# A graph network's aggregation loops: PE drains every four steps, and its sequencer increments the semaphore in place of the matmul

## The chip, the cores and the metric

The kernel runs on one core of one Trainium2 chip. The metric is the time of the program on the device in microseconds. Three runs of the kernel before took 13378.3, 13381.01 and 13399.08 us; their median is 13381.01 us. Within 0.2% of it is 27 us to either side.

## The reference, cut to what matters

```python
def _gcn_layer(x, src, dst, norm, W, b, n_nodes):
    h = x @ W
    msg = h[src] * norm[:, None]
    out = jax.ops.segment_sum(msg, dst, num_segments=n_nodes)
    return out + b

# x: 12500 x 256 float32; 200000 edges, sorted by dst, and a self edge for each node
x = x + gnn(_layernorm(x), edges)         # three _gcn_layer, gelu behind the first two
x = x + experts(_layernorm(x), edges2)    # attention scores on a second graph pick 2 of 4 experts
```

The change lies in the `segment_sum` of the three layers of the first part.

## The kernel before, in words

The nodes are cut into 98 blocks of 128. Their features (256 float32 each) lie scaled in a table in DRAM, `feature_table`, and the sums are collected in SBUF, in `acc`. The edges are listed as 1664 steps of 128 edges; all edges of a step go to one block. `aggregate(l)` runs once in each of three layers over 52 turns of two halves, each of `U` = 16 steps, so a layer has 104 halves and the three have 312. A finishing stage (`finish`, matmuls with the layer's weights) stands behind each. The two halves of `ring` and of `onehot` take turns. For a half:

- POOL (GpSimd) waits until PE has used this half of the ring (`s_used`), copies 16 columns of indices (L687) and issues 16 indirect DMAs (L691), one for a step; each fetches 128 rows of the table into the ring.
- DVE (VectorE) waits for `s_used` as well and makes the 16 one-hot matrices of the half with one operation, L719 (128x2048, both operands in SBUF), which stands in its program behind the sixteen adds of the half before it.
- PE (TensorE) waits for the rows and for the one-hots, then multiplies, step by step, one-hot by rows into PSUM (L708). A float32 matmul is two passes in the records, so a half has 32. Every `Q` = 4 steps it waits for free PSUM (`s_sum`, L707) and tells DVE that four products are there (`s_mm`, L711). Behind the sixteenth it waits for all of them (L712) and increments `s_used` with its sequencer (L713).
- DVE adds each product to its block in `acc` (L734), four at a time behind a wait for `s_mm` (L732), each behind the one before it; the block numbers are loaded every eight steps (L140, called in L730), and `s_sum` is incremented every four (L739).

The semaphore `s_mm` is the only thing that the change touches. The rest of the program is the layout of the edges in front, an attention stage with loops of its own behind the layers (transposes in L1052, indirect DMAs in L1018) and the experts at the end (matmuls in L1382 and L1397).

Of the kernel before, what the change touches and what calls it, by code (L numbers as in the profile page):

```python
# [22 lines left out]
U = 16  # L23
# [25 lines left out]
def build(nc, x, src, dst, gnn_w, gnn_b, w_gat, att_src, att_dst, b_gat, ln_gamma, ln_beta,  # L49
          ew1, eb1, ew2, eb2, edges2, out):  # L50
    N, D = x.shape
# [22 lines left out]
    with ExitStack() as ctx:  # L74
        def sb(name, shape, dt=F32):
            return ctx.enter_context(nc.sbuf_tensor(name, shape, dt))
# [3 lines left out]
        def sem(name):  # L80
            s = nc.alloc_semaphore(name=name)
            phase_sems.append(s)
            return s
# [12 lines left out]
        ps = ctx.enter_context(nc.psum_tensor("ps", [P, 8, 512], F32))  # L96
# [14 lines left out]
        onehot = sb("onehot", [P, 2, U, P])  # L111
# [26 lines left out]
        def load_blocks(which, i, s, n=8, top=NB - 1):  # L138

            _, values = nc.values_load_multi_w_load_instructions(  # L140
                blk[i][0:1, bass.ds(s, n)], engines=[which], min_val=0, max_val=top,
                skip_runtime_bounds_check_because="the table counts blocks of the graph, made on the chip")
            return values
# [525 lines left out]
        ring = work[:].rearrange("p (h u f) -> p h u f", h=2, u=U)  # L669
        G1 = S1 // (2 * U)  # L670
        Q = 4

        def aggregate(l):
            n = f"_l{l}"
            s_row = [sem(f"rows_in{h}" + n) for h in range(2)]
            s_stg, s_tick = sem("indices_staged" + n), sem("pool_tick" + n)
            s_used = sem("ring_half_used" + n)
            s_hot, s_mm, s_add, s_sum = sem("onehots" + n), sem("products" + n), sem("adds" + n), sem("psum_free" + n)
            with nc.Block() as block:
                @block.gpsimd  # L680
                def _(pool):
                    with pool.Fori(0, G1) as g:
                        for h in range(2):

                            pool.wait_ge(s_used, g * 2 + (h + 1))
                            pool.sem_inc(s_tick, 1)
                            nc.gpsimd.tensor_copy(stage[:, h], idx[0][:, bass.ds(g * (2 * U) + h * U, U)]).then_inc(s_stg, 1)  # L687
                            pool.wait_ge(s_stg, g * 2 + (h + 1))
                            pool.sem_inc(s_tick, 1)
                            for k in range(U):  # L690
                                nc.gpsimd.indirect_dma_start(  # L691
                                    out=ring[:, h, k], out_offset=None, in_=table,
                                    in_offset=bass.IndirectOffsetOnAxis(ap=stage[:, h, k:k + 1], axis=0),
                                ).then_inc(s_row[h], 16)

                @block.tensor
                def _(pe):
                    pe.sem_inc(s_used, 2)
                    with pe.Fori(0, G1) as g:
                        for h in range(2):  # L700
                            pe.wait_ge(s_row[h], (g + 1) * (16 * U))
                            pe.wait_ge(s_hot, g * 2 + (h + 1))
                            for k in range(U):
                                bank = (k // 2) % 8
                                if k % Q == 0:

                                    pe.wait_ge(s_sum, g * (2 * U // Q) + (h * U + k) // Q + 1)  # L707
                                mm = nc.tensor.matmul(ps[:, bank, (k % 2) * D:(k % 2 + 1) * D], onehot[:, h, k],  # L708
                                                      ring[:, h, k], start=True, stop=True, skip_group_check=True)
                                if k % Q == Q - 1:  # L710
                                    mm.then_inc(s_mm, 1)  # L711
                            pe.wait_ge(s_mm, g * (2 * U // Q) + (h + 1) * (U // Q))  # L712
                            pe.sem_inc(s_used, 1)  # L713

                @block.vector
                def _(dve):
                    dve.sem_inc(s_sum, U // Q)
                    def hots(g, h):
                        nc.vector.tensor_tensor(  # L719
                            onehot[:, h], iota[:].unsqueeze(1).broadcast_to([P, U, P]),  # L720
                            dloc[0][:, bass.ds(g * (2 * U) + h * U, U)].unsqueeze(2).broadcast_to([P, U, P]),
                            ALU.is_equal).then_inc(s_hot, 1)
                    with dve.Fori(0, G1) as g:
                        for h in range(2):
                            dve.wait_ge(s_used, g * 2 + (h + 1))
                            hots(g, h)
                            for k in range(U):
                                bank = (k // 2) % 8
                                if k % 8 == 0:
                                    base = load_blocks(mybir.EngineType.DVE, 0, g * (2 * U) + (h * U + k), top=(NB - 1) * D)  # L730
                                if k % Q == 0:
                                    dve.wait_ge(s_mm, g * (2 * U // Q) + (h * U + k) // Q + 1)  # L732
                                at = bass.ds(base[k % 8], D)
                                nc.vector.tensor_tensor(acc[:, at], acc[:, at], ps[:, bank, (k % 2) * D:(k % 2 + 1) * D],  # L734
                                                        ALU.add).then_inc(s_add, 1)

                                dve.wait_ge(s_add, h * U + k + 1)
                                if k % Q == Q - 1:
                                    dve.sem_inc(s_sum, 1)  # L739
                        dve.sem_clear(s_add)  # L740
# [262 lines left out]
        s_hot, s_mm, s_mrg, s_keep = sem("gat_penalties"), sem("gat_scores"), sem("gat_merged"), sem("gat_rows_kept")  # L1003
# [465 lines left out]
```

## Time and profile before

| | |
|---|---|
| median of three runs | 13381.01 us |
| the profiled execution's own time: its span | 14933.7 us |
| the same, core 0's mean granted TensorE clock | 0.702 |
| L691, indirect DMAs on POOL | 4992, 5155.3 us busy |
| L708, matmul passes on PE | 9984, 2933.4 us busy |
| L734, adds on DVE | 4992, 2103.8 us busy |
| L719, one-hots on DVE | 312, 716.4 us busy |

The profiled execution lasted 1553 us (11.6%) longer than the median of the runs. Of its own time no other figure is there than its span. A row of the timeline below gives the start in us, the duration in us, the engine, the line, the operation and how many are merged, and in brackets the idle time before it with what ended it. "remote" and "issue" are idle times for which no instruction of another engine is named. The granted clock is in parts of TensorE's full 2.4 GHz.

### The profile page before, as it was taken

The page shows a single profiled execution, that of the slowest core. Times are in us where ns is not written, and L with a number is a line of the kernel's source. Part 1 is how long each engine was busy: PE and PEld are TensorE (multiplying, and loading weights), DVE is VectorE, ACT ScalarE, POOL GpSimd, SP SyncE. Part 2 cuts the span into 40 slices and gives each one's busy share as a digit, 9 for nine tenths or more (in the row PEclk, how much of TensorE's full clock was granted, in tenths as well). Part 3 has the DMA queues.
Part 4 walks back from the last instruction along what each step waited for, and adds up shares of the span by engine and source line. Part 5 has one row for each costly group of instructions (what it writes and reads, how often), then busy time and mean ns, then how long its engine had stood idle before and what let it go on. Part 6 is the DMA issues. An engine that isn't in the chain of part 4 may idle for free. (4 is left out here: it accounts for less than half of the span.)

```text
span 14933.7 us, 122356 instructions
## 1 busy us (share of the span) xinstructions
PE 6795.4 (46%) x29462; PEld 5570.3 (37%) x29462; DVE 6207.0 (42%) x12229; ACT 2112.3 (14%) x6085; POOL 7853.7 (53%) x8847
## 2 busy tenths in 40 slices
PE   0120034333434334343443334336555555777999
PEld 0120023333323333333333333325333334777888
DVE  8870233333333333333333333335444445553222
ACT  0000000000001000000100000003666664111222
POOL 0387367777765777777477777761545554330000
PEclk9997566676667666666666666666555555558999
DMA  0000133333322333333133333323000000001000
GB/s 8 7 0 5 44 103 88 88 88 88 89 68 73 89 87 88 88 87 88 53 88 90 90 88 90 88 65 94 5 5 5 5 5 4 1 1 33 28 29 27
DMA packets 468304, 809.55 MB, mean 54 GB/s; under 512 B 156361, under 2 KB 306425, under 8 KB 468210
## 3 DMA queue, kind: packets, MB, share of 16 engines
q0 software_dynamic: 309248, 667.09, 16.3%
q1 hardware_dynamic: 158962, 141.56, 3.1%
q14 instruction: 79, 0.65, 0.0%
q8 instruction: 15, 0.25, 0.0%
HBM read 729.01 MB, written 79.15 MB: 54 GB/s over the span
## 5 line engine op out<-in xcount | busy, mean ns | idle before, releaser
L691 POOL DMA_INDIRECT work<-feature_table,stage x4992 | 5155.3, 1033 | 1758.4 <-issue 1575.6
L708 PE MATMUL ps<-work,onehot 128*128 128x256 f32 x9984 | 2933.4, 465 | 5150.6 <-DVE onehot L719 2591.1
L708 PEld LDWEIGHTS ps<-work,onehot 128*128 128x128 f32 x9984 | 2367.5, 241 | 5716.4 <-issue 5274.2
L734 DVE TENSOR_TENSOR acc<-acc,ps 128x256 f32 x4992 | 2103.8, 421 | 4472.5 <-PE ps L708 1772.9
L1052 PE MATMUL ps<-ident,onehot 128*128 128x128 f32 x4608 | 1160.9, 402 | 1105.1 <-ACT onehot L1037 435.8
L1037 ACT ACTIVATE onehot<-work 128x128 f32<-128x128 bf16 x4608 | 1374.5, 387 | 801.8 <-DMA HG<-L_ffn_edge_index_in 635.4
L1052 PEld LDWEIGHTS ps<-ident,onehot 128*128 128x128 f32 x4608 | 767.6, 204 | 1498.1 <-issue 770.9
L1018 POOL DMA_INDIRECT work<-attention_table,stage x1152 | 1106.3, 960 | 405.3 <-issue 349.8
L226 POOL DMA_INDIRECT edge_list<-rec_stage,stage x1024 | 1115.7, 1090 | 369.2 <-issue 309.5
L780 ACT ACTIVATE work<-acc,dinv 128x256 f32 (+1 forms) x294 | 131.6, 496 | 7732.1 <-PEq L794 7539.5
L1075 DVE TENSOR_REDUCE work<-ps 128x4 f32<-128x512 f32 x1152 | 720.6, 684 | 885.0 <-DMA HG<-L_ffn_edge_index_in 652.6
L719 DVE TENSOR_TENSOR onehot<-iota,dloc 128x2048 f32<-128x2048 f32 x312 | 716.4, 2296 | 189.9 <-DVE acc L734 107.4
L1382 PE MATMUL ps<-acc 128*128 128x256 f32 x3136 | 703.4, 380 | 68.4 <-DMA acc<-x_normed_t 68.4
L1397 PE MATMUL ps<-acc 128*128 128x256 f32 x3136 | 700.8, 379 | 0.0
L1382 PEld LDWEIGHTS ps<-acc 128*128 128x128 f32 x3136 | 597.5, 191 | 150.2 <-issue 68.6
L1397 PEld LDWEIGHTS ps<-acc 128*128 128x128 f32 x3136 | 595.8, 190 | 81.0
L1247 POOL COPY work<-work 128x24 bf16 x1152 | 274.2, 289 | 648.6 <-PE ps L1206 592.2
L1437 DVE SCALAR_TENSOR_TENSOR acc<-ps,gates,acc 128x256 f32<-128x256 f32 x392 | 171.7, 479 | 963.2 <-PE ps L1397 963.2
L1014 POOL COPY stage<-idx 128x16 int32 x72 | 15.8, 219 | 966.6 <-PEq L1055 677.1
L803 PE MATMUL ps<-gw_sb,work 128*128 128x256 f32 x1176 | 319.2, 420 | 402.4 <-DVE work L824 258.4
L687 POOL COPY stage<-idx 128x16 int32 x312 | 132.1, 423 | 668.5 <-PEq L713 344.7
L1413 ACT ACTIVATE acc<-ps,acc 128x256 f32<-128x256 f32 x784 | 307.6, 475 | 969.0 <-PE ps L1382 969.0
(202 smaller groups left out, 5302.9 us busy)
## 6 DMA issues: line engine op xcount, KB each, us to landing
work<-feature_table,stage POOLq DMA_INDIRECT x4992
feature_table<-acc SPq DMA_DIRECT2D x98, 256.0 KB
work<-attention_table,stage POOLq DMA_INDIRECT x1152
edge_list<-rec_stage,stage POOLq DMA_INDIRECT x1024
feature_table<-acc SPq DMA_DIRECT2D x7, 1792.0 KB, 6.7
x_after_gnn<-acc SPq DMA_DIRECT2D x49, 256.0 KB
x_normed_t<-work SPq DMA_DIRECT2D x49, 256.0 KB, 2.2
acc<-x_normed_t SPq DMA_DIRECT2D x49, 256.0 KB, 2.8
```

The costliest lines, as they stand in the source:

```text
L226: nc.gpsimd.indirect_dma_start(out=target, out_offset=bass.IndirectOffsetOnAxis(ap=stage[0:rows, h, k:k + 1], axis=0), in_=rec_stage[0:row ...
L691: nc.gpsimd.indirect_dma_start(out=ring[:, h, k], out_offset=None, in_=table, in_offset=bass.IndirectOffsetOnAxis(ap=stage[:, h, k:k + 1], ...
L708: mm = nc.tensor.matmul(ps[:, bank, (k % 2) * D:(k % 2 + 1) * D], onehot[:, h, k], ring[:, h, k], start=True, stop=True, skip_group_check= ...
L719: nc.vector.tensor_tensor(onehot[:, h], iota[:].unsqueeze(1).broadcast_to([P, U, P]), dloc[0][:, bass.ds(g * (2 * U) + h * U, U)].unsqueez ...
L734: nc.vector.tensor_tensor(acc[:, at], acc[:, at], ps[:, bank, (k % 2) * D:(k % 2 + 1) * D], ALU.add).then_inc(s_add, 1)
L803: mm = nc.tensor.matmul(ps[:, 2 + r, a * D:(a + 1) * D], zt[:, r, a, k * P:(k + 1) * P], gw_sb[:, l, k], start=(k == 0), stop=(k == KD - 1 ...
L1018: nc.gpsimd.indirect_dma_start(out=grow[:, h, k], out_offset=None, in_=gat_table, in_offset=bass.IndirectOffsetOnAxis(ap=stage[:, h, k:k + ...
L1037: ins = nc.scalar.activation(pairs4[:, k % 4, j], penal[:, h, k], ACT.Identity, bias=grow[:, h, k, HE + j:HE + j + 1], scale=BIG)
L1052: mm = nc.tensor.transpose(ps[:, bank, j * P:(j + 1) * P], pairs4[:, k % 4, j], ident[:])
L1075: nc.vector.tensor_reduce(mx[:, h, k], ps[:, k % 8].rearrange("p (j e) -> p j e", j=NH), AX.X, ALU.max).then_inc(s_pf, 1)
L1382: mm = nc.tensor.matmul(ps[:, 2 * (e % 2) + m // 2, (m % 2) * 2 * P:(m % 2 + 1) * 2 * P], w1[:, e, k, m * P:(m + 1) * P], xt[:, r, :, k], ...
L1397: mm = nc.tensor.matmul(to, hid[:, e % 2, m, a * P:(a + 1) * P], w2[:, e, m], start=(m == 0), stop=(m == KH - 1), skip_group_check=True)
```

## The change

The last matmul of each four no longer increments `s_mm`. PE is drained there instead, and its sequencer increments `s_mm` with an instruction of its own. The wait for `s_mm` before `s_used` falls away.

```diff
                                 if k % Q == 0:
                                     pe.wait_ge(s_sum, g * (2 * U // Q) + (h * U + k) // Q + 1)
-                                mm = nc.tensor.matmul(ps[:, bank, (k % 2) * D:(k % 2 + 1) * D], onehot[:, h, k],
-                                                      ring[:, h, k], start=True, stop=True, skip_group_check=True)
+                                nc.tensor.matmul(ps[:, bank, (k % 2) * D:(k % 2 + 1) * D], onehot[:, h, k],
+                                                 ring[:, h, k], start=True, stop=True, skip_group_check=True)
                                 if k % Q == Q - 1:
-                                    mm.then_inc(s_mm, 1)
-                            pe.wait_ge(s_mm, g * (2 * U // Q) + (h + 1) * (U // Q))
+                                    pe.drain()
+                                    pe.sem_inc(s_mm, 1)
                             pe.sem_inc(s_used, 1)
```

## Rows read from the trace of the kernel before

**Rows 1.** First and third loop: length, PE, PEld, DVE, ACT, POOL busy, PE clock, DMA

```profile
1904.00:4376.00 2472.00, 963.21 (x3296) 778.16 (x3296) 929.74 (x1747) 0.00 (x0) 1758.40 (x1766) 0.69 0.30 88
...
7453.00:9927.00 2474.00, 980.17 (x3328) 790.70 (x3328) 939.68 (x1768) 0.87 (x3) 1761.93 (x1770) 0.68 0.30 88
```

**Rows 2.** One half in which POOL waits for nobody, timeline from 2094 us

```profile
2094.23 0.21 POOL L687 COPY stage<-idx 128x16 int32 x1
...
2096.26 8.86 PE L708 MATMUL ps<-work,onehot 128*128 128x256 f32 x32 [15.34 <-DMA work<-feature_table,stage]
...
2110.32 0.95 POOL L691 DMA_INDIRECT work<-feature_table,stage  x1 [0.30 <-issue]
...
2115.04 0.20 POOL L687 COPY stage<-idx 128x16 int32 x1
```

**Rows 3.** The last half of the third layer, with its adds on DVE

```profile
9911.42 9.53 PE L708 MATMUL ps<-work,onehot 128*128 128x256 f32 x32 [11.26 <-DMA work<-feature_table,stage]
9915.33 2.08 DVE L734 TENSOR_TENSOR acc<-acc,ps 128x256 f32 x4 [5.04 <-PE ps L708]
9917.72 2.08 DVE L734 TENSOR_TENSOR acc<-acc,ps 128x256 f32 x4 [0.31 <-PE ps L708]
9920.84 2.08 DVE L734 TENSOR_TENSOR acc<-acc,ps 128x256 f32 x4 [1.04 <-issue]
9923.24 2.08 DVE L734 TENSOR_TENSOR acc<-acc,ps 128x256 f32 x4 [0.31 <-DVE acc L734]
```

**Rows 4.** The first half of the first layer: adds, POOL and PE, timeline from 1928 us

```profile
1928.14 9.29 PE L708 MATMUL ps<-work,onehot 128*128 128x256 f32 x32 [643.78 <-DMA work<-feature_table,stage]
...
1951.13 2.08 DVE L734 TENSOR_TENSOR acc<-acc,ps 128x256 f32 x4 [10.15 <-remote]
1951.43 0.20 POOL L687 COPY stage<-idx 128x16 int32 x1 [4.53 <-PEq L713]
```

**Rows 5.** Who waited for whom, in total over the span: us, times, longest

```profile
DVE acc L734 <- remote: 1652.7, 314, 13.9
...
POOL stage L1014 <- PEq L1055: 677.1, 69, 15.4
...
POOL stage L687 <- PEq L713: 344.7, 107, 4.6
```

**Rows 6.** The one-hots of L719 between POOL's DMAs, timeline from 1954 and from 2876 us

```profile
1955.94 2.29 DVE L719 TENSOR_TENSOR onehot<-iota,dloc 128x2048 f32<-128x2048 f32 x1 [0.33 <-DVE acc L734]
1956.24 2.81 POOL L691 DMA_INDIRECT work<-feature_table,stage  x1 [0.30 <-issue]
...
1959.35 0.95 POOL L691 DMA_INDIRECT work<-feature_table,stage  x1 [0.30 <-issue]
...
2876.72 2.29 DVE L719 TENSOR_TENSOR onehot<-iota,dloc 128x2048 f32<-128x2048 f32 x1 [0.83 <-DVE acc L734]
2877.94 1.89 POOL L691 DMA_INDIRECT work<-feature_table,stage  x1 [0.30 <-issue]
2880.14 0.95 POOL L691 DMA_INDIRECT work<-feature_table,stage  x1 [0.30 <-issue]
```

**Rows 7.** A drain behind two matmuls, and PE's sequencer: ns min/median/max

```profile
138.90 0.75 PE L412 MATMUL ps<-work,ones 128*128 128x98 f32 x2 [138.90 <-DVE acc L308]
...
L314 PEldq DRAIN  x2: 795/926/1057, 138.9 to 1014.5; - x2
...
L713 PEldq EVENT_SEMAPHORE  x312: 51/51/51, 1951.1 to 9921.0; - x156
L1140 PEldq DRAIN  x1: 8/8/8, 13505.5 to 13505.5; - x1
```

**Rows 8.** Passes and weight loads: of L708 min/median/max, of L1382 sixteen in a row

```profile
L708 PEld LDWEIGHTS ps<-work,onehot x9984: 190/190/338, 1928.1 to 9920.4; 128*128 128x128 f32 x200
L708 PE MATMUL ps<-work,onehot x9984: 379/379/791, 1928.1 to 9920.6; 128*128 128x256 f32 x200
...
14201.32 3.62 PE L1382 MATMUL ps<-acc 128*128 128x256 f32 x16
```

## The prediction

> **What bounds the kernel now.** Read first the busy times by stretch [rows 1]. In a loop of 2472 us POOL is busy for 1758, PE for 963, DVE for 930, and the DMA engines are at 0.30. POOL carries the most, but no engine is full. The third loop has 2474 us, the second is like them: about 7420 us in all, 23.8 for each of 312 halves.
>
> Then the timeline of one half in which POOL waits for nobody [rows 2]. From copy to copy it takes 2115.04 - 2094.23 = 20.81 us: sixteen indirect DMAs, one every 1.254 us, and about a us for the copy. PE starts on the half that was just fetched 2.03 us behind the copy and is done 8.9 us later (2933.4 us over 312 halves is 9.4 on average, by the table of the page). So PE gives a half of the ring back some 11.4 us into the 20.8 that POOL needs for the other one. The reader is to see 9 us of slack there. The last half of the third layer shows DVE [rows 3]: its first adds begin 3.91 us behind PE, then at 6.30, 9.42 and 11.82, and end at 13.9. Group 1 waits for PE; from there DVE, with 2.4 us a group and 3.1 where block numbers are loaded, is mostly the slower.
>
> What makes 23.8 out of 20.8? Two things. The first is L719 [rows 6]. While DVE builds one-hots for 2.29 us, the next DMA of POOL doesn't end. With L719 0.03 us behind the start of a DMA (2877.94 - 1.25 = 2876.69), the next-but-one starts 2.20 us behind the next in place of 1.25: POOL loses 0.95. With L719 0.95 us behind such a start, it loses 3.11 - 1.25 = 1.86. The loss is thus about 0.92 us plus L719's distance from the last start, 0.92 to 2.17 in all. The second is late signals. In the first half PE's records end at 1937.43, and yet the third group's adds begin at 1951.13, behind a wait for "remote", and POOL's copy is released by PE's sequencer only then [rows 4]. Such waits come to 1652.7 us in 314 cases on DVE, about one a half, and they cost POOL 344.7 us in L687 [rows 5].
>
> The median of the runs is 1553 us under this profiled execution. I read the late signals as belonging to the profiled execution for the greater part: POOL without them would need 20.81 + 1.5 = 22.3 us a half, 6960 in all, which gives back 460; another 677.1 are POOL's waits of the same kind in the attention stage [rows 5]; together 1140 of the 1553, with the other stages left for the rest. That the two sums come near to each other is an argument, not a proof, and the first rival stands on its being false. Under this reading the loops of the runs are bound by POOL's issue.
>
> **The change, part by part.** *Removed.* 1248 increments by matmuls, which occupy nobody, and 312 waits of PE's sequencer before L713, which wait for what the last drain now waits for. Nothing is gained on POOL's path. No DMA moves, and no queue is passed by anything.
>
> *Added: 1248 drains, four a half.* A drain that stands behind two matmuls took 795 ns beside 0.75 us of matmuls, so it ended 0.05 us behind them; one with nothing before it took 8 ns [rows 7]. So it waits for the array and adds 0.05. Then the sequencer's increment takes 0.051 us [rows 7]; with what no row shows of its way to DVE I take the signal to be 0.2 us later than the matmul's own, between 0.05 and 0.4. Then the next group starts anew. The pass behind used to start 0.22 us behind its forerunner (sixteen passes take 3.62 us with the last at 0.38), now it starts behind its end: 0.16 lost at 2.4 GHz. Its weights have to be loaded, 0.19 to 0.34, and the first pass is up to 0.79 [rows 8]. With the sequencer's instructions between I take 0.8 us a group, between 0.45 and 1.2. Three of these gaps lie inside a half: PE needs 9.4 + 2.4 + 0.2 = 12.0 us, and gives back its half of the ring 2.0 + 12.0 = 14.0 us into POOL's 20.8. The cover is 6.8 us. If the gaps keep PE at 1.2 GHz all through, each group takes 3.91 [rows 3] and the half 4 x 3.91 + 3 x 0.8 = 18.0, given back at 20.1: still hidden, now by 0.7 us plus L719's loss of 1.5.
>
> The Trainium skill, in "VectorE: DVE Perf Modes", section "The DRAIN you can't avoid", tells of boilerplate drains of about 12 ns on all engines; by it the 1248 drains would cost 15 us at most, and by the 795 ns row they cost what the array still has to do. Either is hidden under POOL here.
>
> *What is late next.* Behind the waits for `s_mm` on DVE stand the adds and, behind them, L719 of the half that PE has just given back. Nobody waits for that one-hot soon (PE needs it 20 us later), but where L719 falls decides what POOL loses. Now: PE starts 2.03 behind the copy, the last adds begin 11.82 later, and L719 follows 2.08 + 0.33 later, or 2.08 + 0.83 where a turn of the loop lies between [rows 3, 6]: 16.3 or 16.8 us behind the copy, up to 0.5 more where group 2 is late. POOL's thirteenth DMA starts at 2110.32 - 2094.23 = 16.09 [rows 2], the next at 17.34. The distances are 0.2 to 0.7 and 0.7 to 1.2, mostly near the low ends; mean 0.57, loss 1.5 us. After: group 1's signal is 0.2 late, group 2 is bound by PE in place of DVE, 0.2 to 1.5 later in all, taken at 0.8. L719 comes at 17.1 to 17.6 and at 17.6 to 18.1. The first lot is astride the start at 17.34 (distance 1.0 to 1.25, and 0 to 0.25), the second at 0.25 to 0.75. Mean 0.53, loss 1.45. The difference of -0.05 us times 312 is -15 us; with the unknown size of the shift it can be 0.15 to either side, 47 us. At 1.2 GHz throughout, L719 falls around the copy at 20.8; for that place no row of mine differs in kind, and I take a loss between 0.92 and 2.17.
>
> *The tails.* The last half of each layer has no POOL to hide it: three times about 2.6 us on PE, of which DVE's own pace hides 1.8: +3 us, bounds 1 and 15.
>
> Sum: 0 (drains and increments) - 15 + 3 = -12 us, with +15 for the chance of a lower clock moving more of L719 to dear places: 13381 + 3. The sum is made on the trace's halves and laid on the median, since what differs between the two executions, the late waits, isn't in it. I say 13385.
>
> The Trainium skill, in "SBUF — State Buffer", section "SBUF: two separate sides", has DVE operations with two SBUF inputs and GpSimd exclude each other for the whole instruction. By a lock that costs the same wherever it falls, the change would be worth nothing but the tails; the two cases above (0.95 and 1.86 us) show that the place matters, so I keep the 47 us.
>
> **The rivals.** *First, faster: the late signals are real.* If the runs have them too, and the sequencer's increment isn't held up as the matmul's is, POOL no longer waits: 344.7 us in L687 [rows 5], giving 13036; it decides once the signals come less than about 9 us late. For it: 314 waits, one a half. Against: 1553 us have to vanish somewhere, and a drain would wait for the same completion. Chance 0.09.
>
> *Second, faster by place.* The shift carries L719 just past the starts of DMAs more often than I think: -0.3 us a half at most by likelihood, 13290; bound 0.57 x 312 = 178 us. Chance 0.13.
>
> *Third, slower by place.* The shift is 0.3 to 0.5, not 0.8, or the clock stays low: then L719 falls late in a DMA's time, loss 1.75 to 2.0, +0.25 to +0.5 us a half, +80 to +156, typically 13480. It decides from a mean shift of +0.09 us. For it: PE's gaps come at a granted clock of 0.69 already [rows 1], between the two levels. Chance 0.28.
>
> *Fourth, slower by the drain.* A gap of over 1.7 us in place of 0.8, at the low clock, makes PE and not POOL the bound; each us more costs 3 x 312 = 936 us. Against it: the 795 ns row. Chance 0.05, from 13600 up.
>
> **How the numbers follow.** No change, within 0.2% (27 us, about what a measurement of this kernel can tell): 0.45. Faster 0.09 + 0.13 = 0.22. Slower 0.28 + 0.05 = 0.33. The range leaves out the first and the fourth rival and the ends of the other two: 13290 to 13530. My own case alone is 13340 to 13430.
>
> **What the profile of the changed kernel would show.** PE should have 1248 more drains, each behind its matmuls and 0.05 us longer, and gaps of 0.5 to 1.2 us between groups of eight passes; the mean half from first to last pass about 12 us. POOL's undisturbed half should stay at 20.8 us, and the first adds come 4.1 us behind PE. DVE's "remote" waits should stay if they belong to the completion of matmuls; if they vanish while the runs don't move, they were the profile's. L719 should begin 17 to 18 us behind the copy in undisturbed halves. I'm wrong if POOL waits for L713 in an undisturbed half, or if the loops' share of the change is over 0.15 us a half.

## The result and the profile after

The changed kernel took 13439.15 us (median of six runs) beside 13386.03 us for the kernel before (six runs): ratio 1.0038, 95% interval 1.0027 to 1.005. It is 53 us slower. The range of 13290 to 13530 holds the time. What the prediction called its own case alone, 13340 to 13430, misses it by 9 us. The likeliest case, no change beyond 0.2%, didn't come, the side of "slower" did (0.33).

The profiled execution of the changed kernel spans 13439.0 us, as long as its runs. The one of before that the prediction read spanned 14933.7 us. Where that difference comes from, the run before_again shows. Two lines of the changed kernel's page:

```profile
span 13439.0 us, 123604 instructions
...
PE 6900.3 (51%) x29462; PEld 5352.4 (40%) x29462; DVE 6241.2 (46%) x12229; ACT 2094.0 (16%) x6085; POOL 7963.1 (59%) x8847
```

Its waits, of which PE's and DVE's in the loops are shown (us in total, times, longest). No wait of L734 is called remote any more, and POOL's L687 waits for no L713 or L712, where it waited 344.7 us [rows 5]:

```profile
PE ps L708 <- DMA work<-feature_table,stage: 4292.8, 312, 408.6
DVE acc L734 <- PEq L711: 3162.4, 488, 26.7
...
PE ps L708 <- issue: 131.0, 611, 0.2
```

What ran is not quite what the program text says. The text asks for a drain (L711) and for an increment of `s_mm` by an instruction of its own (L712). In the trace the 1248 drains carry the increment, and DVE is released by them, as the line above shows. Of sequencer increments there are 312, one behind each half's fourth drain, under L712, and none under L713:

```profile
L712 PEldq EVENT_SEMAPHORE  x312: 51/51/51, 1702.7 to 9132.8; - x156
```

Those are the increments of `s_used`. The 0.051 us that the prediction gave to an increment of `s_mm` don't occur. Where the texts below speak of sequencer increments of PE for `s_mm`, read drains that increment.

One half of the changed kernel in the timeline:

```profile
6002.68 0.21 POOL L687 COPY stage<-idx 128x16 int32 x1
...
6004.65 3.78 PE L708 MATMUL ps<-work,onehot 128*128 128x256 f32 x8 [11.67 <-DMA work<-feature_table,stage]
...
6008.59 2.08 DVE L734 TENSOR_TENSOR acc<-acc,ps 128x256 f32 x4 [9.23 <-PEq L711]
...
6008.65 2.97 PE L708 MATMUL ps<-work,onehot 128*128 128x256 f32 x8 [0.22 <-issue]
...
6011.78 2.08 DVE L734 TENSOR_TENSOR acc<-acc,ps 128x256 f32 x4 [1.11 <-PEq L711]
...
6019.70 2.29 DVE L719 TENSOR_TENSOR onehot<-iota,dloc 128x2048 f32<-128x2048 f32 x1 [0.33 <-DVE acc L734]
6019.99 2.83 POOL L691 DMA_INDIRECT work<-feature_table,stage  x1 [0.30 <-issue]
6023.12 0.95 POOL L691 DMA_INDIRECT work<-feature_table,stage  x1 [0.30 <-issue]
...
6025.32 0.21 POOL L687 COPY stage<-idx 128x16 int32 x1
```

The reader is to see three things. PE's passes now come in packs of eight with 0.22 us between the modelled end of one and the start of the next. POOL goes on from copy to copy without a wait, in 22.64 us here: 20.81 and 1.83 more, for the DMA that L719 stretched to 2.83 us. And L719 stands 17.02 us behind POOL's copy, 0.96 us behind the start of the last DMA (19.99 - 1.25 = 18.74), a dear place.

### The profile page after: what moved, and what is told of

It is laid out like the page before. It is cut to its first block and busy times, and to the rows that moved or that the text cites. A ratio compares the mean times of both kernels' runs of the same rounds, so it can differ in the third digit from the quotient of the medians.

```text
span 13439.0 us, 123604 instructions
## 1 busy us (share of the span) xinstructions
PE 6900.3 (51%) x29462; PEld 5352.4 (40%) x29462; DVE 6241.2 (46%) x12229; ACT 2094.0 (16%) x6085; POOL 7963.1 (59%) x8847
## 5 line engine op out<-in xcount | busy, mean ns | idle before, releaser
L691 POOL DMA_INDIRECT work<-feature_table,stage x4992 | 5235.6, 1049 | 1759.2 <-issue 1486.2
L708 PE MATMUL ps<-work,onehot 128*128 128x256 f32 x9984 | 3126.9, 467 | 4493.0 <-DMA work<-feature_table,stage 4292.8
L708 PEld LDWEIGHTS ps<-work,onehot 128*128 128x128 f32 x9984 | 2209.9, 233 | 5409.7 <-issue 4833.0
L734 DVE TENSOR_TENSOR acc<-acc,ps 128x256 f32 x4992 | 2102.9, 421 | 4125.5 <-PEq L711 3162.4
L1018 POOL DMA_INDIRECT work<-attention_table,stage x1152 | 1196.3, 1038 | 405.0 <-issue 348.0
L1052 PE MATMUL ps<-ident,onehot 128*128 128x128 f32 x4608 | 1113.9, 388 | 562.8 <-ACT onehot L1037 490.3
L1052 PEld LDWEIGHTS ps<-ident,onehot 128*128 128x128 f32 x4608 | 734.4, 197 | 942.0 <-issue 646.8
L719 DVE TENSOR_TENSOR onehot<-iota,dloc 128x2048 f32<-128x2048 f32 x312 | 715.7, 2294 | 323.2 <-DVE acc L734 171.8
L1382 PE MATMUL ps<-acc 128*128 128x256 f32 x3136 | 702.4, 380 | 68.8 <-DMA acc<-x_normed_t 68.8
L1382 PEld LDWEIGHTS ps<-acc 128*128 128x128 f32 x3136 | 596.8, 190 | 150.3 <-issue 68.9
L1413 ACT ACTIVATE acc<-ps,acc 128x256 f32<-128x256 f32 x784 | 307.6, 475 | 968.0 <-PE ps L1382 968.0
L1180 DVE TENSOR_TENSOR acc<-acc,ps 128x20 f32 x1152 | 201.8, 175 | 257.0 <-DVE acc L1180 222.4
L1082 DVE TENSOR_TENSOR emx<-emx,work 128x4 f32 x1152 | 190.5, 165 | 268.6 <-DVE work L1075 124.3
```

Of the source, the lines that this page charges most:

```text
L691: nc.gpsimd.indirect_dma_start(out=ring[:, h, k], out_offset=None, in_=table, in_offset=bass.IndirectOffsetOnAxis(ap=stage[:, h, k:k + 1], ...
L719: nc.vector.tensor_tensor(onehot[:, h], iota[:].unsqueeze(1).broadcast_to([P, U, P]), dloc[0][:, bass.ds(g * (2 * U) + h * U, U)].unsqueez ...
L1018: nc.gpsimd.indirect_dma_start(out=grow[:, h, k], out_offset=None, in_=gat_table, in_offset=bass.IndirectOffsetOnAxis(ap=stage[:, h, k:k + ...
L1052: mm = nc.tensor.transpose(ps[:, bank, j * P:(j + 1) * P], pairs4[:, k % 4, j], ident[:])
L1382: mm = nc.tensor.matmul(ps[:, 2 * (e % 2) + m // 2, (m % 2) * 2 * P:(m % 2 + 1) * 2 * P], w1[:, e, k, m * P:(m + 1) * P], xt[:, r, :, k], ...
L1413: ge = nc.scalar.activation(hid[:, e % 2, m], ps[:, 2 * (e % 2) + m // 2, (m % 2) * 2 * P:(m % 2 + 1) * 2 * P], ACT.Gelu, bias=b1[:, e, m: ...
```

## The experiments

Each experiment ran beside the kernel before on the same chip, and the chips were of two kinds: on some, before takes 13383 to 13386 us, as in the result; on others 14774 to 14793 us, and the trace has late signals as in [rows 4]. Every ratio below is to the kernel before on the same chip, and I call the two kinds punctual and late.

The theories: A, the change costs what L719's later place costs POOL. B, the late signals belong to increments by matmuls and not to the profile. C, it costs by the number of drains or sequencer increments. D, L719's place costs nothing. E, on late chips the drain waits for the late completion and PE with it; F, the drain escapes it. G, the cost goes through PE or its clock.

**before_again** (late chip), the kernel before with no edit.

> The kernel before, unchanged, with a profile of its own. Both theories: the time is that of before within 0.2%, which shows what a comparison can tell. Theory A (place of L719): the profiled execution now lasts about 13385 us, without the late signals; POOL's period is about 22.5 us a half (22.64 in the changed kernel, less 0.16), the second adds of a half begin 6.3 to 6.4 us behind PE's first pass on average against 6.50 in the changed kernel, and L719 begins about 0.15 us earlier behind the copy than its 16.6 to 16.7 us there. Theory B (late signals belong to matmul increments): the profiled execution shows them again, with waits called remote on nearly every half.

Measured: 14793.14 us, ratio 1.0002 (0.9993 to 1.0011); profiled span 14800.3. The same kernel takes 1407 us more here than beside the result, and its waits are those of the trace that I predicted from:

```profile
DVE acc L734 <- remote: 1420.4, 291, 14.0
...
POOL stage L1014 <- PEq L1055: 608.6, 64, 15.2
...
POOL stage L687 <- PEq L713: 314.8, 98, 4.6
```

So the late signals are in the unprofiled runs too, on such a chip. My reading of them as part of the profiled execution is refuted, and with it the forecast of a profile of about 13385 us.

The loops have less than a quarter of the difference. Against the trace of drain_last (below, punctual) this one is longer by 231 us ahead of the first loop, 330 in the three loops, 204 in the finishing stages between them, 644 behind the third loop, and by about 1 in the experts' stage at the end (worked out from the starts of L687 and L1382 and the ends of L734). Nor are only the increments of `s_mm` late: the finishing stage has waits of the same name, up to 32.5 us, which the changed kernel's trace from a punctual chip hasn't:

```profile
DVE work L819 <- remote: 330.7, 14, 32.5
```

**drains_only** (late chip):

```diff
                                 if k % Q == Q - 1:
                                     mm.then_inc(s_mm, 1)
+                                    pe.drain()
```

> Drains every four steps, but the matmuls still increment. Theory A: what costs is the restart of PE behind the first drain, which delays group 2 and by it L719; the signal of the sequencer itself is only 0.02 us later. So nearly all of the change is here: +35 to +55 us. Theory C (the sequencer's increments cost, four a half, through a signal that comes later): less than 15 us of the 53 are here.

Measured: 14978.51 us, ratio 1.0123 (1.01 to 1.0146). On a late chip drains alone cost 186 us, far more than either forecast, both of which were made for a punctual one. By far the greater part of the change's cost is in the drains there, since the whole change costs 1.36% (below); C, which had it in the increments, falls on a late chip.

**late2** and **late9** (late chip): two and nine increments of a spare semaphore by DVE's sequencer, ahead of L719.

```diff
                             dve.wait_ge(s_used, g * 2 + (h + 1))
+                            for _ in range(9):
+                                dve.sem_inc(s_late, 1)
                             hots(g, h)
```

> The kernel before, with two sequencer increments of DVE (about 0.1 us each) ahead of L719 and nothing on PE. Theory A: L719 starts 0.2 us later in each half, POOL loses 0.2 us more in most of 312 halves, +45 to +65 us, like the changed kernel. Rival D (what the change costs lies in PE, not in L719's place): no change, within 15 us, since DVE is free for 8 us a half.

> The kernel before, with nine such increments ahead of L719, about 0.86 us. Theory A: the distance of L719 from the start of POOL's last DMA wraps past 1.254 us in most halves, from about 0.5 to 0.1, so POOL loses less: 0.3 to 0.4 us a half, -60 to -125 us against before. Rival D: no change or a few us more, since the delay is hidden. A rival with a loss that only grows with the delay: +0.86 x 312 = +268 us.

Measured: 14783.88 us, 0.9992 (0.9983 to 1.0001), and 14764.02 us, 0.9985 (0.9976 to 0.9994). Both forecasts missed: late2 gave no loss, late9 22 us of gain by the ratio, where -60 to -125 was expected. Late signals scatter L719 over POOL's half there: in the trace of before_again it starts within 5 us behind a copy in 122 halves and over 16 us behind it in nearly all others, so a delay can't set its distance from a DMA's start; these two runs speak neither for A nor for D on a punctual chip.

**after_again** (late chip), the changed kernel with no further edit.

> The changed kernel, unchanged, beside the kernel before. Where before takes some 13386 us: 1.0038 again (+40 to +65 us). Where before takes some 14790 us, because signals of matmuls come late: theory E (the drain waits for the same late completion, and now PE itself stands in it before each next group) +1% or more, as drains alone gave +1.23% there; theory F (only the increment of a matmul is late, the drain is not) a gain of 2 to 4%, since POOL's waits for L713 vanish.

Measured: 14973.95 us beside 14774.45, ratio 1.0136 (1.0115 to 1.0156). That is theory E; F is refuted. The drains' own durations (ns, min/median/max), first of the changed kernel on the punctual chip, then here:

```profile
L711 PEldq DRAIN  x1248: 1832/1988/3777, 1692.2 to 9130.7; - x179
```

```profile
L711 PEldq DRAIN  x1248: 1970/3738/14452, 1923.7 to 10097.9; - x179
```

A drain lasts as long as the eight passes ahead of it, 1.99 or 3.78 us; on the late chip it lasts up to 14.45. Then PE stands where it would have gone on with the next group, and POOL waits 556.9 us for its half of the ring in this trace, in place of 314.8 in before_again:

```profile
POOL stage L687 <- PEq L712: 556.9, 121, 11.3
```

The timeline of that trace shows PE standing 7.14 us between two groups:

```profile
6001.56 1.99 PE L708 MATMUL ps<-work,onehot 128*128 128x256 f32 x8 [0.27 <-issue]
...
6010.64 2.08 DVE L734 TENSOR_TENSOR acc<-acc,ps 128x256 f32 x4 [7.06 <-PEq L711]
...
6010.69 3.78 PE L708 MATMUL ps<-work,onehot 128*128 128x256 f32 x8 [7.14 <-issue]
```

**drain_first** (late chip): as drains_only, but one drain a half, where `k == Q - 1`.

> The kernel before with one drain a half, behind the fourth step; all increments by matmuls. Theory A where signals are punctual: group 2 is the one whose signal binds DVE, so this drain alone costs most of the change, +30 to +55 us. Rival C (sequencer increments cost): 0. Where signals are late: below the +1.23% of four drains, about a quarter of it, since the wait behind the first group is the one that is least often late.

Measured: 14813.31 us, ratio 1.0029 (1.0017 to 1.0041), a quarter of four drains' 1.23%, as expected for a late chip.

**act_hots_before** and **act_hots_after** (late chip, twice each): ACT makes the one-hots and L719 is gone from DVE. The core of the edit; act_hots_after has the change's drains and increments besides.

```python
act.wait_ge(s_used, g * 2 + (h + 1))
nc.scalar.activation(negated[:, h], dloc[0][:, bass.ds(g * (2 * U) + h * U, U)],
                     ACT.Copy, scale=-1.0).then_inc(s_neg, 1)
act.wait_ge(s_neg, g * 4 + (2 * h + 1))
for k in range(U):
    far = nc.scalar.activation(onehot[:, h, k], iota[:], ACT.Abs, bias=negated[:, h, k:k + 1])
far.then_inc(s_neg, 1)
act.wait_ge(s_neg, g * 4 + (2 * h + 2))
nc.scalar.activation(onehot[:, h].rearrange("p u m -> p (u m)"),
                     onehot[:, h].rearrange("p u m -> p (u m)"),
                     ACT.Relu, bias=ones[:, 0:1], scale=-1.0).then_inc(s_hot, 1)
```

> The kernel before, but ACT makes the one-hots (sixteen Abs of iota minus the place, then one Relu of 1 minus it), DVE has no L719. Theory A (L719's overlap costs POOL 0.92 to 2.17 us a half): where signals are punctual POOL's period falls from 22.5 to 20.81 us, 312 x 1.7 = -530 us, about 12860. Rival D (L719 costs POOL nothing on the path): within 30 us of before. Where signals are late: -300 to -530 us.

> The same with the change's drains and sequencer increments. Theory A: with L719 gone there is nothing that a later DVE could push, so the change costs only its tails: within 10 us of act_hots_before where signals are punctual. Rival G (the change costs through PE, its sequencer or the granted clock): 40 to 60 us more than act_hots_before, as on the kernel before.

Measured: 14743.9 us, ratio 0.9979 (0.997 to 0.9987), and 15497.1 us, ratio 1.049 (1.0475 to 1.0504). The gain of 300 to 530 us didn't come, but the stretched DMAs went. Here are POOL's indirect DMAs (ns, min/median/max), with L719 on DVE in before_again and then without it in act_hots_before:

```profile
L691 POOL DMA_INDIRECT work<-feature_table,stage x4992: 942/946/3063, 1901.0 to 9833.9; - x200
```

```profile
L693 POOL DMA_INDIRECT work<-feature_table,stage x4992: 942/949/1007, 1898.5 to 9764.4; - x200
```

Not one of the 4992 is over 1.01 us any more, and a half in which POOL waits for nobody takes 20.77 us, though PE, DVE and now ACT work beside it:

```profile
6018.24 0.20 POOL L689 COPY stage<-idx 128x16 int32 x1 [4.94 <-PEq L715]
...
6039.01 0.20 POOL L689 COPY stage<-idx 128x16 int32 x1
```

So it is L719 on DVE that stretches the DMAs: with the same one-hots made on ACT, and all else of the loop in place, none is stretched. The time stays because on a late chip POOL waits instead: 700.0 us for PE's increment of `s_used`, in place of 314.8. ACT's first operation of a half waits for PE instead (4180.4 us in 235 cases), and DVE for signals (3002.1 us, 368 cases, longest 20.3):

```profile
ACT negated L722 <- PEq L715: 4180.4, 235, 32.4
DVE acc L745 <- remote: 3002.1, 368, 20.3
```

Theory A's forecast of +10 us at most for the drains, made for a punctual chip, isn't tested by this. The drains cost far more with ACT's one-hots, 15497 against 14744; they last up to 18.9 us:

```profile
L713 PEldq DRAIN  x1248: 1923/3352/18927, 1917.5 to 10547.9; - x179
```

**after_late9** (punctual chip): late9's edit on the changed kernel.

> The changed kernel with nine sequencer increments of DVE ahead of L719, which start it 0.84 us later. Theory A where signals are punctual: the distance from POOL's last DMA start goes from mostly 0.5 to 1.2 us on by 0.84 and past 1.254 in nearly all halves, to 0.1 to 0.8; POOL loses 0.3 to 0.5 us less a half, -95 to -155 us against the changed kernel, which makes it 40 to 100 us faster than before. Rival D (L719's place costs nothing): +50 us against before, as the change alone. Where signals are late: within 0.3% of the changed kernel there, +1.1 to +1.6% against before.

Measured: 13365.45 us beside 13383.41, ratio 0.9984 (0.9975 to 0.9993). The changed kernel goes from 1.0038 to 0.9984 by nothing but idle instructions on DVE: 72 us, where 95 to 155 was forecast. It beats the kernel before by 18 us (0.16%), where 40 to 100 was forecast. A has the direction, with sizes forecast too large; rival D is refuted. L719 stands 0.77 us later on average than in the changed kernel (17.45 us behind the copy against 16.69), and POOL loses 0.21 us less a half, 67 of the 72 us (worked out over 306 halves as below). Its timeline, another half than the ones above:

```profile
6006.11 0.95 POOL L692 DMA_INDIRECT work<-feature_table,stage  x1 [0.30 <-issue]
6006.35 2.29 DVE L720 TENSOR_TENSOR onehot<-iota,dloc 128x2048 f32<-128x2048 f32 x1 [1.63 <-issue]
6007.36 2.10 POOL L692 DMA_INDIRECT work<-feature_table,stage  x1 [0.30 <-issue]
6009.76 0.94 POOL L692 DMA_INDIRECT work<-feature_table,stage  x1 [0.31 <-issue]
```

The one-hots stand 0.24 us behind the DMA's start and the next DMA lasts 2.10, not 2.83: POOL loses 1.15 us (2.40 from start to start less 1.25), not 1.88 (3.13 less 1.25) as in the half of the changed kernel above.

**drain_last** (same punctual chip): one drain a half, at its end, which carries the increment as in the changed kernel.

```diff
-                                if k % Q == Q - 1:
+                                if k % Q == Q - 1 and k < U - 1:
                                     mm.then_inc(s_mm, 1)
-                            pe.wait_ge(s_mm, g * (2 * U // Q) + (h + 1) * (U // Q))
+                            pe.drain()
+                            pe.sem_inc(s_mm, 1)
```

> The kernel before with one drain and one sequencer increment a half, behind the sixteenth step, in place of that matmul's increment and of the wait before L713. Theory A where signals are punctual: DVE is behind PE there, and PE has nothing to start, so within 10 us of before. Rival C (sequencer increments or drains cost by their number): a quarter of the change, +13 us. Theory E where signals are late: PE waited for that completion before too, so within 0.15% of before, against +1.23% for drains behind all four groups. Rival F (the drain escapes the late completion): a gain of over 1%.

Measured: 13385.15 us, ratio 0.9997 (0.9988 to 1.0006). One drain with its increment where nothing follows is free within the noise; a cost by number of a quarter of the change (+0.1%) is only just outside the interval. The profile of this kernel is the nearest that I have to one of before on a punctual chip. Its three loops and POOL's busy time in them (windows from the first copy of a layer to its last add; the columns as in [rows 1]):

```profile
1669.00:4018.00 2349.00, 958.34 (x3328) 776.59 (x3328) 939.09 (x1768) 0.00 (x0) 1744.27 (x1767) 0.69 0.32 93
4193.00:6559.00 2366.00, 979.60 (x3328) 790.80 (x3328) 939.18 (x1768) 0.00 (x0) 1761.02 (x1768) 0.69 0.32 92
6735.00:9092.00 2357.00, 975.23 (x3328) 788.40 (x3328) 939.01 (x1768) 0.00 (x0) 1751.92 (x1767) 0.69 0.32 93
sum 7072.00, PE 2913.17 PEld 2355.78 DVE 2817.28 ACT 0.00 POOL 5257.20; mean PE 971.06 PEld 785.26 DVE 939.09 ACT 0.00 POOL 1752.40
```

The same of the changed kernel:

```profile
1668.00:4040.00 2372.00, 1037.08 (x3328) 733.92 (x3328) 939.01 (x1767) 0.00 (x0) 1767.62 (x1768) 0.72 0.32 92
4216.00:6586.00 2370.00, 1045.26 (x3328) 738.74 (x3328) 939.65 (x1768) 0.00 (x0) 1765.09 (x1768) 0.72 0.32 92
6762.00:9136.00 2374.00, 1044.52 (x3328) 737.27 (x3328) 939.31 (x1768) 0.00 (x0) 1768.95 (x1768) 0.72 0.32 92
sum 7116.00, PE 3126.86 PEld 2209.93 DVE 2817.97 ACT 0.00 POOL 5301.66; mean PE 1042.29 PEld 736.64 DVE 939.32 ACT 0.00 POOL 1767.22
```

The loops are 44 us longer of the 49 by which the spans differ (13439.0 and 13390.4), and POOL's busy time is longer by the same 44 us (5301.66 - 5257.20), DVE's by less than 1. The time is inside POOL's DMAs, and what lengthens those is L719, as act_hots_before showed. That speaks against G too: PE is 214 us longer busy in these loops, but POOL waits for it in neither.

**act_hots_before_2** and **act_hots_after_2** repeated the ACT pair, for a punctual chip, and met a late one.

> One-hots made by ACT, increments by the matmuls, once more, for a chip on which signals are punctual. Theory A there: POOL's period falls from the 22.5 us of the run with one drain a half to 20.81 us, 312 x 1.69 = -527 us, about 12860; POOL's DMAs are 0.95 us in every half. Rival D: within 30 us of before. Where signals are late: -0.2% again.

> The same with the change's drains and sequencer increments. Theory A where signals are punctual: PE is 9.4 to 10.6 us busy of 20.81 a half and no L719 is there to be pushed, so within 15 us of the run above. Rival G (the change costs through PE, its sequencer or the granted clock and not by L719's place): +40 to +60 us on the run above. Where signals are late: +4.9% again, by theory E.

Measured: 14758.25 us, ratio 0.9977 (0.9968 to 0.9986), and 15501.03 us, ratio 1.048 (1.0465 to 1.0494). They repeat the late result. What taking L719 away gives in time on a punctual chip wasn't measured.

## Why the prediction was right or wrong, step by step

In short: the range held the time, but the sign was missed. It held because it was wide enough for the third rival; the prediction's own sum, and its point of 13385, were not borne out.

**What bounds the loops: right where the result was measured.** POOL's issue does, at 20.81 us a half and L719's toll. In the changed kernel POOL waits for no L712 in L687. The toll has the form that was read off two halves. In each of the three punctual traces the DMA behind the one in whose time L719 starts ends 3.11 us behind L719's start (3.10 to 3.12 in nine halves of ten). Without L719 it would end 2.20 us behind the start of the DMA ahead (1.25 and 0.95), so the loss is 0.91 us plus L719's distance. Over 306 halves of each trace, distance and loss above 20.81 us from copy to copy come to 0.623 and 1.69 (drain_last), 0.742 and 1.83 (changed), 0.502 and 1.62 (after_late9), worked out from the starts of L687, L691 and the one-hots. From copy to copy the loss is 0.85 us plus the distance in most halves. One gap of 2.22 us in place of 0.30 after each 112 DMAs adds 0.27 a half in all three; the prediction's 22.3 us a half lacked it, and 22.5 was measured in drain_last.

**Late signals: wrong.** "I read the late signals as belonging to the profiled execution" fails: before_again has them at an unprofiled 14793 us. Trace and median that I was given came from chips of different kinds. The numbers that I took over from the undisturbed halves held, since a late chip's punctual halves run like a punctual chip's.

**Drains and increments: hidden, as forecast, and taken too dear.** I took the signal to be 0.2 us later: DVE's first adds begin 3.93 us behind PE in place of 3.91, and 0.16 in place of 0.13 us behind the modelled end (medians), so 0.02 to 0.03. The drain itself ends 0.02 us behind the last pass. I took 0.8 us a group for the restart: from first pass to last PE now needs 10.66 us on average against 9.34 in drain_last, 1.33 for three restarts, 0.44 each, just under my lower bound of 0.45. Given back at about 12.8 us of 22.6, it is hidden.

**The place of L719: the term with the wrong size, and by it the wrong sign.** I shifted it by 0.8 us in all halves and let the early lot pass the next DMA's start, for -15 us. The smaller restart shows in one half of a turn only. In the first half of a turn PE's second group now ends 6.55 us behind PE's start in place of 5.95, later than DVE is ready for it; the second adds begin at 6.72 in place of 6.35, and the L719 behind them stands 16.70 us behind the copy in place of 16.34. Its distance is 0.80 in place of 0.55, and POOL's half is 0.22 longer. In the second half of a turn PE's second group ends at 5.96 in place of 5.81, still ahead of DVE, whose own pace hides the restart: L719 stands at 16.67 in place of 16.73, and POOL's half is 0.06 longer. (All are means over 153 halves, against drain_last.) Over both, L719 is 0.155 us later. Single halves scatter by more than that: the distance is larger in 181 of 306 and smaller in 110, so the cost is one of the mean. It is 0.14 us a half, 43 us in 312. "Group 2 is bound by PE in place of DVE" was thus right for half of the halves, and the shift too large by five times on the mean. A shift too small to pass the next start was the third rival, from a mean of +0.09 us a half on; it came with 0.14 and 45 to 53 us, under the 80 that I gave as its least, and 0.14 is just under the 0.15 at which I would have called the case wrong.

**The tails** took 0.6 us more than in drain_last (+3 forecast); they lie inside the 44 us. Of the other 5 us by which the spans differ 4 come behind the third loop, where the two programs are alike; no cause is shown for them.

**The first rival, that sequencer increments escape the late signals,** was wrong where the lateness is real: the drain waits for the same completion, and the change costs 1.36% there.

**The clock** didn't fall: 0.72 in the changed kernel's loops against 0.69 in drain_last's. PE was busy longer and the clock no lower, so the low clock's part in the third and fourth rivals is refuted on the punctual chip.

**The lock:** the prediction set the place of L719 against the exclusive lock of the Trainium skill ("SBUF — State Buffer", section "SBUF: two separate sides"). That section has the lock, where DVE has two SBUF inputs, only against a GpSimd operation that reads SBUF, a condition that the prediction left out; POOL's DMAs here take their indices from `stage`, which lies in SBUF. The two don't disagree. The DMA that is under way when L719 starts ends on time (0.94 to 0.96 us in all three traces), and the next ends 3.11 us behind L719's start, 0.82 behind its end, wherever L719 stood. Under such a fixed end the toll must depend on the place, by up to 1.25 us; "a lock that costs the same wherever it falls" was not a form that this lock could take. Which port or queue holds the DMA up no run here shows.

**What stays open:** why one chip signals a matmul's completion up to 14 us late, and what else makes it slower outside the loops. The two kinds share the program; in the experts' stage, where no indirect DMA runs, ACT's waits for L1382 are the same on both (969.4 and 968.0 us). Whether the indirect DMAs cause it wasn't tried. Also open are the time of the ACT pair on a punctual chip, which of the four drains costs what there, and why L719's place scatters from half to half.

## What to carry to other kernels

When an engine with slack is made later, ask what its operations block while they run, not only who waits for their results: here 0.155 us of mean shift on DVE, with 8 us of slack, cost POOL 0.14 us a half. The toll of this collision grows with the distance behind a DMA's start and falls back by 1.25 us at the next start, so a delay can also earn: measure one delayed version before building on the order as found. And when the span of a profile and the median of the runs differ by 10%, run the unchanged kernel again before explaining the difference away.

## What the runs showed of the hardware that I hadn't expected

The same program takes 13386 us on some chips and 14790 us on others. The matmuls' pace is the same (a half takes PE 9.38 us in before_again, 9.34 in drain_last), but increments of `s_mm` come up to 14 us late, and three quarters of the difference lie in other stages. A drain doesn't get round that: its median goes from 1988 to 3738 ns and its longest to 14452 ns.

A drain that increments signals only 0.02 to 0.03 us later than the matmul's own increment, and PE's restart behind it costs 0.44 us a group. While DVE runs the 2.29 us of L719 (a `tensor_tensor` with both inputs in SBUF), POOL finishes the indirect DMA that it is in and ends the next one 3.11 us behind L719's start; sixteen Abs and a Relu on ACT that make the same one-hots leave all 4992 DMAs at 0.94 to 1.01 us. POOL's indirect DMAs have a gap of 2.22 us in place of 0.30 once in 112.
